# Quads 1 and 2 summed over adj's sides in float32r passes, in three of four groups

## The reference, cut to what matters

```python
def _L1_gnn_ref(x, W, adj, bias):
    adj_0 = jnp.diag(jnp.diagonal(adj))
    adj_1 = jnp.triu(adj, k=1)
    adj_2 = jnp.tril(adj, k=-1)
    h = jnp.einsum('bjf,kfo->kbjo', x, W)
    out = (jnp.einsum('ij,bjo->bio', adj_0, h[0]) + jnp.einsum('ij,bjo->bio', adj_1, h[1])
           + jnp.einsum('ij,bjo->bio', adj_2, h[2]))
    return out + bias[None, None, :]

h = relu(layernorm(x))
x = x + _L0_gnn_ref(h, adj, ...)   # two graph layers, then LSTMs over windows of 1, 2, 3 and 4 positions
h = relu(layernorm(x))
x = x + _L1_gnn_ref(h, L1_gnn_W, adj, L1_gnn_bias)
```

## Time and profile before

| | |
|---|---|
| median of 3 runs | 393.39 us (393.28 to 394.52) |
| the profiled execution | 394.06 us, its span 391.6 us |
| TensorE matmuls | busy 386.2 us, 99% of the span |
| TensorE weight loads | 341.1 us, 87% (beside matmuls) |
| VectorE | 334.4 us, 85% |
| ScalarE | 279.9 us, 71% |
| GpSimd | 64.2 us, 16% |
| granted TensorE clock | full (2.4 GHz) in all slices of the span |

### The profile page before, as it was taken

How to read it: one execution, slowest core, us unless ns; L and a number is a source line. 1 busy time by engine, 2 the same in 40 slices (tenths; PEclk the granted TensorE clock), 3 DMA queues, 4 the chain that set the end, 5 groups by cost and what they waited for, 6 DMA issues and landing times.

```text
span 391.6 us, 6502 instructions
## 1 busy us (share of the span) xinstructions
PE 386.2 (99%) x2346; PEld 341.1 (87%) x2346; DVE 334.4 (85%) x867; ACT 279.9 (71%) x556; POOL 64.2 (16%) x67
## 2 busy tenths in 40 slices
PE   8999999999999999999999999999999999999996
PEld 8787899997976889899777889899897788989986
DVE  6669999998988788897998888989798958778895
ACT  4768776876597786777389777777659868667563
POOL 4820200101440003001043000300134000000242
PEclk9999999999999999999999999999999999999999
DMA  6940000005282000122366000030529200000045
GB/s 203 381 191 3 0 0 2 1 2 107 39 140 68 0 28 0 38 98 54 56 109 136 27 2 28 2 134 2 110 27 190 53 0 28 0 28 1 4 77 163
DMA packets 12559, 24.76 MB, mean 63 GB/s; under 512 B 4720, under 2 KB 6000, under 8 KB 11632
## 3 DMA queue, kind: packets, MB, share of 16 engines
q0 software_dynamic: 3600, 10.49, 15.1%
q1 hardware_dynamic: 8928, 13.87, 10.2%
HBM read 16.99 MB, written 4.22 MB: 54 GB/s over the span
## 4 chain that ended last, share of the span: by engine, by line
PE 59%; DVE 5%; DMA 1%; issue 1%; ACT 1%; POOL 1%; DVEq 0%; POOLq 0%
PE PS L612 9%; PE PS L613 9%; PE PS L628 8%; PE PS L659 5%; PE PS L648 5%; PE PS L649 5%; PE PS L708 4%; PE PS L552 2%; PE PS L529 2%; PE PS L562 2%; PE PS L700 2%; PE PS L544 2%; PE PS L701 2%; PE PS L702 2%; DMA X<-bias_row 1%
## 5 line engine op out<-in xcount | busy, mean ns | idle before, releaser
L975 ACT ACTIVATE GT<-PS,BG 128x256 f32<-128x256 f32 (+2 forms) x312 | 158.4, 564 | 16.0 <-PE PS L659 12.5
L612 PE MATMUL PS<-HH,WIH 128*128 128x256 f32 (+2 forms) x312 | 106.2, 341 | 0.3 <-DVE X L1241 0.3
L613 PE MATMUL PS<-HH,WIL 128*128 128x256 f32 (+2 forms) x312 | 102.7, 330 | 0.0
L628 PE MATMUL PS<-HL,WIH 128*128 128x256 f32 (+2 forms) x287 | 94.5, 329 | 0.0
L990 ACT ACTIVATE TC<-CS 128x512 f32<-128x512 f32 (+2 forms) x88 | 44.9, 510 | 45.9 <-DVE CS L1121 33.8
L612 PEld LDWEIGHTS PS<-HH,WIH 128*128 128x128 f32 x312 | 58.7, 188 | 10.0 <-DVE HH L1162 4.2
L430 POOL TENSOR_TENSOR RS<-VE,NHALF 128x4 f32<-128x4 f32 (+2 forms) x18 | 34.0, 1888 | 202.5 <-DVE VE L1057 131.4
L613 PEld LDWEIGHTS PS<-HH,WIL 128*128 128x128 f32 x312 | 58.8, 188 | 4.1 <-issue 1.2
L648 PE MATMUL PS<-SH,WHH 128*128 128x256 f32 (+2 forms) x192 | 59.9, 313 | 0.0
L649 PE MATMUL PS<-SH,WHL 128*128 128x256 f32 (+2 forms) x192 | 59.6, 311 | 0.0
L659 PE MATMUL PS<-SL,WHH 128*128 128x256 f32 (+2 forms) x189 | 59.0, 312 | 0.0
(11 more groups left out here) (107 smaller groups left out, 646.6 us busy)
## 6 DMA issues: line engine op xcount, KB each, us to landing
out_tbd<-X SPq DMA_DIRECT2D x15, 256.0 KB, 2.0
X<-x_tbd SPq DMA_DIRECT2D x3, 1024.0 KB, 11.8
H<-x_dbt SPq DMA_DIRECT2D x3, 1024.0 KB, 5.7
H<-HF POOLq DMA_DIRECT2D x6, 512.0 KB, 4.7
X<-bias_row POOLq DMA_DIRECT2D x6, 512.0 KB, 6.9
H<-means POOLq DMA_DIRECT2D x6, 256.0 KB, 5.1
H<-means POOLq DMA_DIRECT2D x3, 512.0 KB, 5.7
WI<-wih_t SPq DMA_DIRECT2D x1, 1024.0 KB, 5.6
```

Of the source, the lines that this page charges most:

```text
L612: pe.matmul(dst, WIH[:, p - 1, cols], x_high, start=True, stop=False)
L613: pe.matmul(dst, WIL[:, p - 1, cols], x_high, start=False, stop=False)
L628: mm = pe.matmul(dst, WIH[:, p - 1, cols], x_low, start=False, stop=(j == 0))
L975: act.activation(GT[:, s, q, 0:n], bank(s, q)[:, 0:n], ACT.Tanh if q == C else ACT.Sigmoid, bias=BG[:, 4 * (p - 1) + q:4 * (p - 1) + q + 1 ...
```

## The change

Quads 1 and 2 (PARTED) of groups 0, 1 and 2 are summed by `parted_sum`: six float32r passes of 512 columns, for each side the high and low parts of adj with the values' high part, then the high parts of adj with the values' low part. Quads 0 and 3 of these groups, and all of the last group, keep the float32 sum.

- ScalarE rounds the values' two side products, in halves of two batches (128 x 2 x 256), into VP (`high_part`): behind the gates of units 6 and 7 for quad 1 and 10 and 12 for quad 2, ahead of that unit's tanh.
- VectorE subtracts (`low_part`): late in units 6, 10 and 12, and mid in unit 7, in the place of quad 1's own term.
- Quad 1's own term moves from mid of unit 7 to mid of unit 8, its addition from mid of unit 8 to mid of unit 9.
- adj's sides are split once in the first turn, on ScalarE behind unit 18 and on VectorE behind unit 19 (128x256 each); the last group's turn and the tables START and STEADY stay.
- TensorE waits for both rounded halves ahead of the first four passes and for both low halves ahead of the last two. ScalarE waits for the low parts before it overwrites the values, and for quad 1's sum before it overwrites VP.

```diff
--- before.py
+++ after.py
@@ -89,6 +89,9 @@
 
 LOW, OWN, ADD = "low", "own", "add"
 LAST = QUADS - 1
+PARTED = (1, 2)
+PART = "part"
+HIGH_PART_AT = {6: (1, 0), 7: (1, 1), 10: (2, 0), 12: (2, 1)}
 
 
 START = {(1, 3): (Piece(SUM, -1, 0, None),),
@@ -103,8 +106,9 @@
 TURN_AT = {(1, 1): 0, (4, 1): 1, (6, 2): 2, (10, 0): 3}
 START_F = {6: (SUM, 0), 7: (VALUE, 6), 10: (VALUE, 9), 11: (VALUE, 10), 12: (VALUE, 11)}
 START_BETWEEN = {0: ((LOW, 0),), 14: ((ADD, 2),)}
-START_MID = {0: ((OWN, -1),), 1: ((ADD, -1),), 4: ((LOW, 1),), 5: ((ADD, 0),), 7: ((OWN, 1),), 8: ((ADD, 1),), 12: ((OWN, 2),)}
-START_LATE = {4: ((OWN, 0),), 5: ((LOW, 2),), 9: ((LOW, 3),)}
+START_MID = {0: ((OWN, -1),), 1: ((ADD, -1),), 4: ((LOW, 1),), 5: ((ADD, 0),), 7: ((PART, (1, 1)),), 8: ((OWN, 1),),
+             9: ((ADD, 1),), 12: ((OWN, 2),)}
+START_LATE = {4: ((OWN, 0),), 5: ((LOW, 2),), 6: ((PART, (1, 0)),), 9: ((LOW, 3),), 10: ((PART, (2, 0)),), 12: ((PART, (2, 1)),)}
 STEADY = Plan(
     at={**START, (12, 3): (Piece(VALUE, 12, 1, (FORGET, 11)),), (13, 3): (Piece(VALUE, 13, 0, (FORGET, 12)),),
         (15, 1): (Piece(VALUE, 14, 0, (VALUE, 13)),), (16, 3): (Piece(VALUE, 15, 1, (SUM, 2)),)},
@@ -122,6 +126,11 @@
 
 
 
+def parted_before(g, q, half):
+
+    return 2 * (len(PARTED) * g + PARTED.index(q)) + half
+
+
 def present(g, n):
 
     return g > 0 or n >= 0
@@ -133,9 +142,9 @@
     return plan is not None and (k in (9, 15) or plan is SECOND and k == 4)
 
 
-LATE_HIGH_AT = {6: ("wi",), 7: ("wh",), 16: ("wl",)}
-LATE_LOW_AT = {7: ("wi",), 9: ("wh",), 18: ("wl",)}
-LATE_ORDER = ("wi", "wh", "wl")
+LATE_HIGH_AT = {6: ("wi",), 7: ("wh",), 16: ("wl",), 18: ("adj",)}
+LATE_LOW_AT = {7: ("wi",), 9: ("wh",), 18: ("wl",), 19: ("adj",)}
+LATE_ORDER = ("wi", "wh", "wl", "adj")
 
 CELL_EARLY = (1, 2, 15)
 FIRST_CELL_EARLY = (1, 2, 3, 15)
@@ -192,6 +201,9 @@
         WHL = sb("WHL", [D, 3, 4 * D], F32R)
         ADJ = sb("ADJ", [T, T])
         ADJ2 = sb("ADJ2", [T, SIDES, T])
+        VP = sb("VP", [T, 2, SIDES * PACK * D], F32R)
+        ADJH = sb("ADJH", [T, SIDES, T], F32R)
+        ADJL = sb("ADJL", [T, SIDES, T], F32R)
         DIAG = sb("DIAG", [T, 1])
         WG0 = sb("WG0", [D, D])
         WG1 = sb("WG1", [D, D])
@@ -286,6 +298,8 @@
         turn_low = sem("turn_low")
         value_mm = sem("value_mm")
         value_sb = sem("value_sb")
+        part_high = sem("part_high")
+        part_low = sem("part_low")
         own_ready = sem("own_ready")
         out_mm = sem("out_mm")
         stored = sem("stored")
@@ -317,11 +331,21 @@
                 return WI[:, POOL_SKIPS, :], WIH[:, POOL_SKIPS, :], WIL[:, POOL_SKIPS, :]
             if what == "wh":
                 return WH[:, POOL_SKIPS - 1, :], WHH[:, POOL_SKIPS - 1, :], WHL[:, POOL_SKIPS - 1, :]
+            if what == "adj":
+                return ADJ2[:, :, :], ADJH[:, :, :], ADJL[:, :, :]
             return WL1[:, :, :], WLH[:, :, :], WLL[:, :, :]
 
         def values(q):
 
             return (WI, WH)[q % 2]
+
+        def parts_of(n):
+
+            return VP[:, n, :].rearrange("p (k e) -> p k e", k=SIDES)
+
+        def halves_of(ap, half):
+
+            return ap[:, :, half * HALF * D:(half + 1) * HALF * D]
 
         def quad(q):
             return slice(q * PACK, (q + 1) * PACK)
@@ -710,6 +734,18 @@
                 if k == SIDES - 1 and (hi == PACK or (g == GROUPS - 1 and q == LAST)):
                     mm.then_inc(out_mm, 1)
 
+            def parted_sum(g, q, ps):
+
+                high, low = parts_of(0), parts_of(1)
+                pe.wait_ge(part_high, parted_before(g, q, 1) + 1)
+                for k in range(SIDES):
+                    pe.matmul(ps[:, :], ADJH[:, k, :], high[:, k, :], start=(k == 0), stop=False)
+                    pe.matmul(ps[:, :], ADJL[:, k, :], high[:, k, :], start=False, stop=False)
+                pe.wait_ge(part_low, parted_before(g, q, 1) + 1)
+                for k in range(SIDES):
+                    mm = pe.matmul(ps[:, :], ADJH[:, k, :], low[:, k, :], start=False, stop=(k == SIDES - 1))
+                mm.then_inc(out_mm, 1)
+
             def last_sum(g, q, ps, lo=0, hi=PACK):
 
                 for k in range(SIDES):
@@ -736,6 +772,8 @@
                     wait_read(after, g)
                 if what == VALUE:
                     last_value(g, n, bank(s, F))
+                elif n in PARTED:
+                    parted_sum(g, n, bank(s, F))
                 else:
                     last_sum(g, n, bank(s, F))
 
@@ -887,6 +925,8 @@
                 if what == "wi":
                     act.wait_ge(w_ih, 16)
                     act.wait_ge(w_hh, 16)
+                elif what == "adj":
+                    act.wait_ge(consts, 6)
                 else:
                     act.wait_ge(w_late, 32)
                 act.activation(high, w, ACT.Copy).then_inc(late_high, 1)
@@ -913,6 +953,9 @@
                 if b == 0 and QUADS * g + q >= 2:
 
                     act.wait_ge(own_ready, QUADS * g + q - 1)
+                    before = QUADS * g + q - 2
+                    if before % QUADS in PARTED and before // QUADS < GROUPS - 1:
+                        act.wait_ge(part_low, parted_before(before // QUADS, before % QUADS, 1) + 1)
                 if g == GROUPS - 1 and b == 0:
                     act.wait_ge(rs2, STREAMS * g + q + 1)
                 elif n % HB == 0:
@@ -921,6 +964,14 @@
                 act.activation(values(q)[:, 0:PARTS, b * D:b * D + D],
                                ps[:, 0:PARTS * D].rearrange("p (k e) -> p k e", k=PARTS), ACT.Copy,
                                scale=RS2[:, n:n + 1]).then_inc(value_sb, 1)
+
+            def high_part(g, q, half):
+
+                act.wait_ge(value_sb, G * g + q * PACK + (half + 1) * HALF)
+                if half == 0 and PARTED.index(q):
+                    act.wait_ge(out_mm, QUADS * g + PARTED[PARTED.index(q) - 1] + 1)
+                act.activation(halves_of(parts_of(0), half), halves_of(values(q)[:, 1:PARTS, :], half),
+                               ACT.Copy).then_inc(part_high, 1)
 
             def last_copy(piece, g):
 
@@ -986,6 +1037,8 @@
                     done = n // 2
                     act.wait_ge(half_cell, IN_HALVES.index(k) + 1)
                     act.activation(TC[:, s, 0:done], CS[:, s, 0:done], ACT.Tanh).then_inc(half_tanh, 1)
+                if plan and k in HIGH_PART_AT:
+                    high_part(i - 1, *HIGH_PART_AT[k])
                 act.wait_ge(cell_ready, len(UNITS) * i + k + 1)
                 act.activation(TC[:, s, done:n], CS[:, s, done:n], ACT.Tanh).then_inc(tanh_ready, 1)
 
@@ -1240,6 +1293,12 @@
                 part = slice(g * G + q * PACK + lo, g * G + q * PACK + hi)
                 dve.tensor_tensor(X[:, part, :], as_batches(ps)[:, lo:hi, :], X[:, part, :],
                                   ALU.add).then_inc(out_ready, 1)
+
+            def low_part(g, q, half):
+
+                dve.wait_ge(part_high, parted_before(g, q, half) + 1)
+                dve.tensor_tensor(halves_of(parts_of(1), half), halves_of(values(q)[:, 1:PARTS, :], half),
+                                  halves_of(parts_of(0), half).bitcast(F32), ALU.subtract).then_inc(part_low, 1)
 
             def late_split_low(what):
 
@@ -1283,6 +1342,9 @@
 
             def last_step(what, g, q, plan):
 
+                if what == PART:
+                    low_part(g, *q)
+                    return
                 if not present(g, q):
                     return
                 if what == LOW:
```

## The result

| | before | after |
|---|---|---|
| median | 393.67 us (4 runs, 393.28 to 394.52) | 397.51 us (4 runs, 396.78 to 397.67) |
| ratio | | 1.0089, 95% interval 1.0071 to 1.0106 |
| the profiled execution, its span | 394.06, 391.6 | 396.78, 394.9 |
| TensorE / VectorE / ScalarE busy | 386.2 / 334.4 / 279.9 us | 385.8 / 341.5 / 286.2 us |

A forecast was written before the change was run, and what follows sets the result against it. TensorE carries 59% of the chain, but casts hold units 9 and 15, so shorter sums gain nothing. Costs 2.07 + 1.34 + 0.34 = 3.75 us on the 393.39 median give 397.1 us, 0.95% slower; range 395.2 to 398.5.

The forecast's parts named there:

- The sums return nothing: Quads 1 and 2: six passes save 0.32 us per sum, 1.9 in all, but casts hold units 9 and 15; gain 0.0.
- some 0.4 and 1 us: Sign in the changed trace: TensorE idle behind each parted sum, about 0.4 us before unit 9, about 1 before unit 15.
- The wait at batch 10: TensorE waits for quad 1's moved addition before writing batch 10's value: 0.69 us a turn, 2.07 in three turns.
- The push at unit 12: VectorE's uncovered subtraction behind unit 12 delays unit 13's product and cast: 0.50 us in two turns, 0.34 in the last, 1.34 together.
- The rival of stalls that swallow one another: VectorE catches up by unit 13 after batch 10's wait, hiding the push at unit 12: 395.8 us; chance 9%.
- adj's split: First turn: VectorE's subtraction behind unit 19 shifts unit 20's output and the transposes by 0.34 us; ScalarE's rounding behind unit 18 nothing.
- ScalarE's roundings: 12 activations of 0.62 us, each before a unit's tanh where ScalarE waits 0.75 us for the cell: cost 0.
- the subtractions of units 6, 7 and 10: VectorE: covered by waits for gates at units 6 and 10 and by the own term's old slot at unit 7: cost 0.
- The Trainium skill's rule on VectorE's pipe: Next operation starts only once the pipe empties: 0.08 us more per inserted operation and the one ahead, about 0.7; not followed.
- The sum: Whole kernel: 2.07 + 1.34 + 0.34 = 3.75 us slower with nothing gained, forecast 397.1 us.

The follow-up runs named there:

- e6: e5 with float32 sums on the unrounded values that wait for the values alone, roundings and subtractions kept unread; 393.66 us, ratio 0.9994.
- e9: e5 with batch 9's value alone moved from inside unit 9 to directly behind quad 1's sum; 393.87 us, ratio 1.0002.
- e1: The kernel before with only quad 1's own term and addition each moved one unit later; 396.31 us, ratio 1.0056.
- e2: The changed kernel with quad 1's addition back behind its own term at mid of unit 8; 395.45 us, ratio 1.0038.
- e8: The kernel before with batch 9's value moved directly behind quad 1's sum and batch 14's behind quad 2's; 393.84 us, ratio 0.9995.
- e5: The changed kernel with the edits of e2 and e3 together; 393.79 us, ratio 0.9997.
- e4: The changed kernel with the six passes replaced by two float32 matmuls on unrounded values, all roundings, subtractions and waits kept; 397.47 us, ratio 1.0085.
- e7: e5 with batch 9's value moved directly behind quad 1's sum and batch 14's behind quad 2's; 393.03 us, ratio 0.9980.
- e10: e9 with float32 sums on the unrounded values; 393.48 us, ratio 0.9991.
- e11: e7 with quad 2's addition moved from behind unit 14's output to behind unit 14's cell; 392.02 us, ratio 0.9959.
- e3: The changed kernel with quad 2's second subtraction moved from behind unit 12 to behind unit 13's cell; 396.25 us, ratio 1.0057.
- e12: e11 with float32 sums on the unrounded values; 392.42 us, ratio 0.9967.

## Why the prediction was right, step by step

*The sums return nothing.* Right, at both places (e6). The passes run 0.23 us apart, six in 1.40. Behind them the array stood from 233.65 to 233.97 before unit 9 and from 256.1 to 257.1 before unit 15; some 0.4 and 1 us were written. What I had not seen is that the casts are only the near end of it: VectorE's own work, the new subtractions in it, bounds the way from batch 8 to 15 (e9), so in two of three turns even a filled gap pays nothing while that order stands.

*The wait at batch 10.* Right to the hundredth: 0.69 us in each of three turns, 2.07 in all. e1 makes it out of the order alone, e2 takes it away.

*The push at unit 12.* Mechanism right: 253.46 to 254.06 is the 0.6 between subtraction and product. Size somewhat over: 0.50, 0.50 and 0.34 written, 0.41 and 0.46 in the table and 0.31 in the last turn (37.43 less 37.02, less the 0.10 of batch 10's record): 1.2 us instead of 1.34. The product was 0.49 later against its turn, but the cast only 0.45: before, the two operations behind the product started 0.46 and 0.54 us apart, now 0.42 and 0.53.

*The rival of stalls that swallow one another* was a piece of the truth. The push costs 0.6 us when the wait at batch 10 is gone (e2) and 0.43 beside it. I had argued that VectorE is late by the same amount behind the wait, and against before it is (unit 12's output 0.70 us later). What I had at nothing is the 0.13 us by which the new work makes VectorE late at unit 12 once the wait is gone: the wait swallows that, and not the push. Mending the wait alone is therefore worth less than its term.

*adj's split.* The first transposes start at 90.97 instead of 90.65. Absolute starts differ between executions (90.72 in e1 and 90.92 in e8, which have no split), so I count from unit 19's last operation on VectorE: 88.02 to 90.97 is 2.95 us, 88.04 to 90.65 is 2.61, and e1 and e8 have 2.61 too. That is the 0.34 written; TensorE of the changed kernel, beside the earlier trace rows:

```profile
90.97 1.20 PE L693 MATMUL PS<-IDENT,HF 128*128 128x128 f32 x8 [0.28 <-DVE HF L1211]
```

Later in the same trace 0.33 us are gained back: from batch 15's value to the following turn's first it is 40.36 us in the profile of before and 40.03 in that of after, 40.03 in e5, 40.33 in e1 and 40.48 in e8, the two that have no split. One turn later before has 40.02 as well, so the gain falls in one turn only. It shows in the waits as TensorE idle for its own issue (1.5 us there before, 1.4 after) and for ScalarE's relu (0.6 before, 0.3 after) in the graph layers. What in the program makes it stays open; no run took the split alone.

*ScalarE's roundings, and the subtractions of units 6, 7 and 10, at nothing.* Right within what e5 can tell.

*The Trainium skill's rule on VectorE's pipe* (VectorE: DVE Perf Modes, "The DRAIN you can't avoid"). That section of the Trainium skill adds that a next operation which is not held starts earlier, and I had left that out. The trace agrees with my rows, not with the longer spacing: the subtraction that lasts 0.69 us is followed by the product 0.60 us later (253.46, 254.06). The 0.7 us more that the rule would have given were not there.

*The sum.* Together the terms are 2.07 + 1.2 + 0.34, less 0.33 that came back: 3.3 us, and the span of the profiled execution grew by 3.3. The median grew by 3.84, with an interval of 2.8 to 4.2. So the mechanism was right, and that the 3.75 of the sum lies within 0.1 of the medians' difference is in part luck: the push came out 0.16 smaller, a gain that I did not see took back 0.33, and the spread of the executions made up for both.

## What to carry to other kernels

A faster operation pays only if something waits for its end; read the start of what follows it, and ask who released that. When an operation is moved by one place to make room, look up every wait on its semaphore on all engines: the two moved entries cost 2.1 us here, all 26 new operations of ScalarE and VectorE 1.5, of which 0.3 came back. A bank that is freed later stops the next writer, and all that is queued behind it. If a shortening leaves a hole, put other work in, and then look again which engine sets the pace. And when a new order gains, try it on the old operations as well: what the order alone is worth in full stayed open here.

## What the runs showed of the hardware

The executions of one kernel spread over more than a microsecond (e5: 393.18 to 394.63). One source is seen in the profile of e2, which had 396.37 us against its median of 395.45: in the third turn ScalarE waited for the DMA that adds the means, a wait that the profile of before doesn't have there. ScalarE of e2 in order of time:

```profile
297.15 0.63 ACT L940 ACTIVATE HTH<-H 128x512 fp32r<-128x512 f32 x1 [1.49 <-DMA H<-means]
```

In that trace the stretch from the third turn's first value to batch 8's is 25.50 us; it is 24.11 in before. The same wait is 1.9 us in all in the profile of e9, 1.8 in e4, 1.2 in e7, 0.8 in e1, at most 0.4 in e5, e8, e10, e11 and after, and absent in before, e3, e6 and e12. It falls on one execution and not on another, and one profile alone would have misjudged e2 by a microsecond; the stretches of the table are free of it, and agree to 0.05 us between kernels that should be alike.
